# State-space scan: where the input rows of a batch's last eight units come from

## The reference, cut to what matters

```python
def _L0_attn_ref(x, log_lambda, Wd, bd, WB, WC, Wout, bout):
    lam = softplus(log_lambda)                                  # D x N
    delta = softplus(einsum('bld,ed->ble', x, Wd) + bd)
    Bt = einsum('bld,nd->bln', x, WB)
    Ct = einsum('bld,nd->bln', x, WC)
    A_d = exp(-delta[..., None] * lam)                          # b, l, D, N
    B_d = delta[..., None] * Bt[:, :, None, :]
    def step(h, inp):                                           # over l
        a, b, c = inp
        h = a * h + b
        return (h, h * c[:, None, :])
    _, ys = lax.scan(step, zeros((B, D, N)), (A_d, B_d, Ct))
    flat = ys.reshape(B, L, D * N)
    return einsum('blk,dk->bld', flat, Wout) + bout
```

## Time and profile before

| | us |
|---|---|
| median of 3 runs | 4217.18 |
| profiled execution | 4220.45 |
| its span | 4218.7 |
| state-space stage | about 279 to 1120 |
| PE, DVE, POOL, ACT busy between 500 and 600 us | 98.99, 89.12, 74.67, 56.93 |

### The profile page before, as it was taken

The page is one execution under the profiler, slowest core; times in us unless marked ns, Lnnn a source line. Parts: engine busy times, 40 slices in busy tenths (PEclk is TensorE's granted clock), DMA queues, the critical chain, the costliest instruction groups (busy, mean ns, idle before and its releaser), DMA issues. The chain is left out here.

```text
span 4218.7 us, 68490 instructions
## 1 busy us (share of the span) xinstructions
PE 3466.4 (82%) x22579; PEld 2664.5 (63%) x22628; DVE 3413.9 (81%) x6252; ACT 2597.1 (62%) x5081; POOL 1864.5 (44%) x2267
## 2 busy tenths in 40 slices
PE   0149999999689999999999686888868887456998
PEld 0039999999589999999999551111112222446998
DVE  7948888888767777777776777999979887885886
ACT  4745555555344444444444477999979998554665
POOL 5757777777534333343333002222232111464665
PEclk9999999999789999999999675555559999557999
DMA  4334445455422122222222248000011112237986
GB/s 116 106 87 140 139 138 139 138 138 156 120 89 93 65 79 96 96 96 76 68 93 89 63 140 333 22 24 26 26 42 47 47 47 56 73 116 210 274 267 176
DMA packets 288617, 458.27 MB, mean 109 GB/s; under 512 B 45619, under 2 KB 223362, under 8 KB 274814
## 3 DMA queue, kind: packets, MB, share of 16 engines
q1 hardware_dynamic: 268350, 428.16, 33.4%
q0 software_dynamic: 18944, 25.85, 2.1%
q10 hardware_dynamic: 1024, 0.54, 0.1%
HBM read 355.23 MB, written 105.12 MB: 109 GB/s over the span
## 5 line engine op out<-in xcount | busy, mean ns | idle before, releaser
L1056 POOL TENSOR_TENSOR c_ap<-c_ac,c_ap 128x420 fp32r<-128x420 f32 x340 | 405.8, 1194 | 724.5 <-ACT c_ap L1247 724.5
L729 PE MATMUL b_pA<-ab_woutT,b_ys 128*105 128x192 f32 x3840 | 691.7, 327 | 4.8 <-POOL b_ys L567 4.2
L729 PEld LDWEIGHTS b_pA<-ab_woutT,b_ys 128*105 128x105 f32 x3840 | 612.4, 172 | 16.1 <-POOL b_ys L567 5.0
L567 POOL TENSOR_TENSOR b_ys<-b_hs,b_cb 128x525 f32<-128x525 f32 x384 | 506.6, 1320 | 227.3 <-DVE b_hs L794 177.0
L1968 DVE TENSOR_REDUCE g_raw<-g_pS 128x1 f32<-128x525 f32 x816 | 549.5, 703 | 31.5 <-PE g_pS L1923 30.2
L1944 ACT ACTIVATE g_pS<-g_pS,g_stt 128x525 f32<-128x525 f32 x816 | 553.7, 777 | 19.7 <-POOL g_stt L1897 18.8
L1923 PE MATMUL g_pS<-g_qk 16*128 16x262 bf16 (+1 forms) x1536 | 461.5, 408 | 94.1 <-ACT g_pS L1944 35.0
L794 DVE TENSOR_TENSOR_SCAN b_hs<-b_ae,b_pB 128x525 f32<-128x525 f32 x384 | 479.3, 1248 | 43.1 <-ACT b_ae L668 7.3
L1247 ACT ACTIVATE c_ap<-c_ac 128x420 fp32r<-128x420 f32 x340 | 189.3, 557 | 524.8 <-DVE c_ac L1445 522.6
L1129 PEld LDWEIGHTS c_pD<-cw_wd,c_ap 128*105 128x105 f32 x4080 | 424.7, 172 | 30.2 <-POOL c_ap L1056 21.3
L1129 PE MATMUL c_pD<-cw_wd,c_ap 128*105 128x192 f32 x4080 | 436.2, 256 | 9.0 <-POOL c_ap L1056 9.0
(11 more groups left out here) (417 smaller groups left out, 7685.5 us busy)
## 6 DMA issues: line engine op xcount, KB each, us to landing
b_cb<-dram_ct SPq DMA_DIRECT2D x64, 1050.0 KB, 6.1
b_cb<-dram_ct SPq DMA_DIRECT2D x64, 525.0 KB
dram_slots<-g_empty SPq DMA_DIRECT2D x33, 772.0 KB, 21.1
cw_spare<-dram_wt SPq DMA_DIRECT2D x20, 1260.0 KB, 10.4
cw_spare<-dram_wt SPq DMA_DIRECT2D x20, 1050.0 KB, 8.9
cw_spare<-dram_wt SPq DMA_DIRECT2D x20, 840.0 KB, 6.3
m_wo_r<-in_L_ffn_wo_dram SPq DMA_DIRECT2D x24, 576.0 KB
o_wo_r<-in_L_ffn_wo_dram SPq DMA_DIRECT2D x24, 576.0 KB, 5.6
```

The source lines that it names most:

```text
L567: pool.tensor_tensor(ys[:, u % RING, :], hs[:, u % RING, :], cb[:, g % 3, u % GU, :], ALU.mult).then_inc(s["ys"], 1)
L729: ins = pe.matmul(into, ys[:, u % RING, t * TP:(t + 1) * TP], woutT[:, u % NU, :], start=(u == 0 and t % 2 == 0), stop=(u % NU == NU - 1), ...
L1056: nc.gpsimd.tensor_tensor(ap[LO][:, r, :], ac[:, r, :], ap[HI][:, r, :].bitcast(F32), ALU.subtract)\
```

## The change

The tail no longer uses `spread`. `ct` grows from 16 to 48 rows: ACT's copy to `cs`, and its DMA, now take 48 partitions (64 to 111), which hold Bt in fp32 (rows 0 to 15), unused rows, and Ct (rows 32 to 47). A new SBUF buffer `bb` has the eight input rows of the tail, as [128, 2, 4, 525] fp32. SP fills it by four more DMAs per batch of 64 partitions each, two behind the `cb` load of group 2 and two behind that of group 3. In the tail, DVE weighs `bb` in place and scans from it, where it did both on `pB`. In units 0 to 15 nothing of this changes. The wait of `br` (L758 before) is now for the semaphore of the `cs` copy, which follows the `bs` copy on ACT.

```diff
@@ ssm @@
+    INPUT_AT = {2: 0, 3: 1}
+    B0, C0 = 64, 32
...
+        bb = sb("bb", [128, (NU - NS) // GU, GU, S])
...
+                    if g in INPUT_AT:
+                        q = INPUT_AT[g]
+                        for t in range(2):
+                            src = ct_d[b, 2 * q * GU:2 * (q + 1) * GU, :].rearrange("(n t) l -> t n l", t=2)
+                            sp.dma_start(bb[64 * t:64 * t + 64, q, :, :],
+                                         src[t:t + 1].broadcast_to([64, GU, S])).then_inc(s_bb[q], 16)
...
                 if half == 0:
-                    a_eng.wait_ge(s["B"], at(b, NU, -NU))
+                    a_eng.wait_ge(s["B"], at(b, NS, -NS))
                 a_eng.activation(bs[:, k, lo:hi], pF[0:96, 0:hi - lo], ACT.Copy).then_inc(s["b1"], 1)
                 if half == 0:
                     a_eng.wait_ge(s_ct[k], i * 32)
-                a_eng.activation(cs[96:96 + NS, k, lo:hi], pF[96:96 + NS, 0:hi - lo], ACT.Copy)\
+                a_eng.activation(cs[B0:B0 + C0 + NS, k, lo:hi], pF[B0:B0 + C0 + NS, 0:hi - lo], ACT.Copy)\
                     .then_inc(s["faR"], 1)
...
-                a_eng.dma_start(ct_d[b, :, lo:hi], cs[96:96 + NS, k, lo:hi]).then_inc(s_ct[k], 16)
+                a_eng.dma_start(ct_d[b, :, lo:hi], cs[B0:B0 + C0 + NS, k, lo:hi]).then_inc(s_ct[k], 16)
...
-                pe.wait_ge(s["hs"], at(b, NU, u + 1 - 2))
+                pe.wait_ge(s["hs"], at(b, NU, u - 1 if u > 1 else NS - 1 + u - NU))
...
-                    if u < NU - 2:
+                    if u < NS - 2:
                         spread(b, k, u + 2)
-                    elif not last:
+                    elif u >= NU - 2 and not last:
                         spread(b + 1, 1 - k, u + 2 - NU)
...
-                dve.wait_ge(s["b1"], at(b, 2, half + 1))
+                dve.wait_ge(s["faR"], at(b, FS, step + 1))
...
+            def inputs(u):
+                return pB[:, u % 2, OFF:OFF + S] if u < NS else bb[:, (u - NS) // GU, (u - NS) % GU, :]
+
             def weigh(b, k, u):
...
-                dve.wait_ge(s["B"], at(b, NU, u + 1))
-                v.tensor_tensor(pB[:, u % 2, OFF:OFF + S], delta[:, k, 0 if u < NS else 1, :], pB[:, u % 2, OFF:OFF + S],
-                                ALU.mult).then_inc(s["bm"], 1)
+                if u < NS:
+                    dve.wait_ge(s["B"], at(b, NS, u + 1))
+                elif (u - NS) % GU == 0:
+                    dve.wait_ge(s_bb[(u - NS) // GU], b * 32 + 32)
+                x = inputs(u)
+                v.tensor_tensor(x, delta[:, k, 0 if u < NS else 1, :], x, ALU.mult).then_inc(s["bm"], 1)
...
-                    v.tensor_tensor_scan(hs[:, u % RING, :], ae[:, u % RING, :], pB[:, u % 2, OFF:OFF + S], 0.0,
+                    v.tensor_tensor_scan(hs[:, u % RING, :], ae[:, u % RING, :], inputs(u), 0.0,
                                          ALU.mult, ALU.add).then_inc(s["hs"], 1)
```

More of the change, by code:

```diff
@@ L462, in ssm @@
         s_ct = [sem(f"s_ct{k}") for k in range(2)]
+        s_bb = [sem(f"s_bb{q}") for q in range((NU - NS) // GU)]
         s_out = [sem(f"s_out{k}") for k in range(2)]
@@ L494, in body @@
                     if g * GU < NS:
-                        src = ct_d[b, g * GU:(g + 1) * GU, :].rearrange("(a n) l -> a (n l)", a=1)
+                        src = ct_d[b, C0 + g * GU:C0 + (g + 1) * GU, :].rearrange("(a n) l -> a (n l)", a=1)
                         sp.dma_start(cb[:, g % 3, :, :].rearrange("p n l -> p (n l)"),
@@ L500, in body @@
                         for t in range(2):
-                            src = ct_d[b, 2 * j:2 * j + 2 * GU, :].rearrange("(n t) l -> t n l", t=2)
+                            src = ct_d[b, C0 + 2 * j:C0 + 2 * j + 2 * GU, :].rearrange("(n t) l -> t n l", t=2)
                             sp.dma_start(cb[64 * t:64 * t + 64, g % 3, :, :],
                                          src[t:t + 1].broadcast_to([64, GU, S])).then_inc(s_cb[g % 3], 16)
+                    if g in INPUT_AT:
[4 more added lines that the diff above has]
+                                         src[t:t + 1].broadcast_to([64, GU, S])).then_inc(s_bb[q], 16)
                     if g == 3 and not first:
@@ L2997, in trunk @@
                             ssm_lam, ssm_wd, ssm_bd, ssm_wb, ssm_wc, ssm_wout, ssm_bout, W)
-            ssm(nc, h0, W, dram("ct", (NB, 16, S)), h1, early["load"])
+            ssm(nc, h0, W, dram("ct", (NB, 48, S)), h1, early["load"])
         dense_experts(nc, early, dense_held, h1, gate_w, gate_b, gate_bias, wu, bu, wg, bg, wd, bd, swu, sbu, swg, sbg, swd, sbd,
```

## The result

The kernel after takes 4358.5 us (median of 4 runs, 4345.6 to 4391.4) against 4219.9 before. The ratio is 1.0345, with a 95% interval of 1.0310 to 1.0379. I had forecast 4325, in a range of 4285 to 4370. The direction and the mechanism were right; the size was 33 us short, and 4358.5 is also above the forecast's own range, 4300 to 4345. (PE is TensorE, DVE VectorE, ACT ScalarE, POOL GpSimd.) Lines have shifted in kernel.py: the weigh is L802 (was L785), the scan L810 (L794), POOL's ys L577 (L567), the projection L739 (L729), the spread L729 (L719), the front pieces L768 and L777 (L758 and L767), POOL's two others L560 and L551 (L550 and L541).

The account below looks back on a forecast made before the run. Heads were taken as PE-paced, tails as DVE-paced. Fifteen batches at +6.7 us plus 7.4 for the last gave +108, other edits 0: 4220.5 to 4328 profiled, median 4325 us, range 4285 to 4370.

Parts of the forecast that it names:

- PE's 29 us: Tails, 16 batches: eight spreads of 0.23 us each leave PE, 29 us in all, buying almost nothing because DVE is last.
- rival 2: Whole kernel: PE's saved 29 us count in full, giving 4188 us; chance 0.04.
- DVE's wait of 0.61 us for unit 16: Start of each tail: DVE's wait for the spread before its weigh disappears, -0.61 us per batch.
- Two SBUF inputs exclude POOL: Tail: paired weighs and scans take turns with POOL's SBUF work, next starting about 0.14 us before the holder's end; +108 us.
- rival 1: Tail: the scan doesn't exclude POOL, only weigh and ys do; 4207 to 4217 us, most likely 4215; chance 0.10.
- The ledger of a tail: Tail: DVE's and POOL's exclusive holds of 25.0 us plus 0.9 of gaps, 25.9 against 18.6; net +6.7 us per batch.
- steady unit: One tail unit: weigh 0.55, ys 1.16, scan 1.11, gap 0.05, together 2.87 us against 1.94.
- The last batch: Final tail, without front work: eight units at 2.87 us instead of 1.94, +7.4 us.
- POOL's late wait for cb: Batch 15: could shrink by 3 us after a longer tail or grow by a few; counted 0, +-5 in all.
- The other edits: L758's new wait, four more DMAs and the 48-partition copy: 0; the wait bounded by 0.4 us per batch, 6 us.
- rival 3: PE's clock falls in the tail's gaps and each head begins slowly, 2.5 us a batch, +40: 4365 us; chance 0.11.
- My 1.2 us: Tail: PE's predicted idle gaps between pieces of work of 1.6 us, far shorter than 4 us.

Follow-up runs that it names:

- e5: The kernel after, with PE still making the tail's eight spreads into PSUM, where nobody reads them: 4342.6 us, ratio 1.0345.
- e6: The kernel before, with input rows of units 8 to 15 from memory, copied to PSUM by ACT instead of spread by PE: 4217.9 us, ratio 1.0033.
- e3: The kernel before, with only the tail's weigh writing its product to SBUF, so the scan has two SBUF inputs: 4300.0 us, ratio 1.0186.
- e8: The kernel after, with POOL's ys of units 16 to 23 on half the columns: 4285.3 us, ratio 1.0206.
- e2: The kernel after, with the tail's weigh writing to PSUM, so only the weigh has two SBUF inputs: 4318.1 us, ratio 1.0274.
- e7: The kernel after, with POOL's three bias additions moved from units 14, 17, 20 to units 9, 11, 13: 4317.2 us, ratio 1.0284.
- e1: The kernel after with its transfers and waits, but tail spreads back on PE and the broadcast rows unused: 4228.2 us, ratio 1.0025.
- after_again: The kernel after, unchanged, run and profiled again: 4350.8 us, ratio 1.0348.

## Why the prediction was right, and where it was short

1. **Heads PE-paced, tails DVE-paced; PE's 29 us buy nothing.** Right. Keeping the spreads (e5) changes no tail. In a kernel without pairs (e6) the relief is worth 0.9 us a batch, so rival 2's 1.84 (29 us over 16 batches) was too much even there. A spread also costs less than my 0.23 us: eight fewer take 1.3 us off PE's busy time, 0.17 each.
2. **DVE's wait of 0.61 us for unit 16 goes.** Right: heads of 33.00 for 33.62 in the mean of fifteen, -0.62.
3. **Two SBUF inputs exclude POOL, the scan too.** Right, and rival 1 is out: in e3 the scan alone is paired and takes 1.81 us in the median, and in e8 it shortens with POOL's work. The Trainium skill's rule (SBUF — State Buffer, Who interferes with whom) holds for tensor_tensor_scan as for tensor_tensor in this kernel. What I took from it for the length of the block, one instruction, is too short: the loser waited for POOL's whole unbroken run (3.31 us in e2, behind two ys and L560).
4. **The ledger of a tail: 25.9 us.** This is the mis-sized term: 27.17 were measured. Its steady unit of 2.87 was exact (e7). The entry "POOL's L550 behind unit 16, L541 behind units 17 and 20" was too small: it lacked the addition of unit 14, which POOL, coming out of the head with a backlog, does inside the tail, and it assumed that the two engines take turns, where DVE waits for POOL's whole run. Without the three additions the tail is 24.8. They cost 2.35, and I had counted 1.2 for two: 1.15 of the missing 1.3. Over 15 batches the period grew by 15 x 7.97 = 119.5 us instead of 101. The last batch gave only 0.5 instead of 7.4. Up to its last scan its tail grew by 7.3, as the ledger has it. But before, PE still had 27 records of projections to start when that scan ended, and after only 14, so 1.4 us of it went again: 5.9. And its head shrank by 5.4, because DVE's waits there, 5.3 us before (3.3 for spreads, the 0.6 of step 2 among them, and 2.0 for ys), are none after. They stand behind POOL's late wait for cb, 7.6 us before and 4.3 after, which I had allowed for in words (3 us) and not in the sum. Stage: +120, forecast +108.
5. **The other edits: 0.** In the kernel after nothing of them is seen. With DVE at its old pace L768's wait costs 5.9 us, the bound given (e1).
6. **The clock (rival 3).** It fell, and it cost nothing. The timeline of PE at the tail's end:

```profile
578.04 0.62 PE L729 MATMUL b_pB<-b_bs,ab_sel 96*128 96x263 bf16 x2 [4.82 <-DVE b_bs L777]
578.45 3.41 PE L739 MATMUL b_pA<-ab_woutT,b_ys 128*105 128x192 f32 x10
...
581.65 0.65 PE L729 MATMUL b_pB<-b_bs,ab_sel 96*128 96x263 bf16 x2
```

The granted clock is 0.87 in the tail and 1.00 in the head. The short gaps did not do it: from 564 to 572 us, with gaps of 0.2 and 1.6, it is 1.00. It fell in a gap of 4.8, to 0.53 from 578 to 583, near the lower of its two levels (1.2 of 2.4 GHz), and is 1.00 again from 583 to 590. My 1.2 us had missed that gap: PE's queue stands at the next batch's spread, which waits for DVE's L777, itself blocked (1.83 for 0.42). The slow projection of 3.41 us lies where DVE sets the pace: between 577 and 584 us DVE has one wait, 0.2 us for ACT, and none for PE.

7. **What stands beyond the stage.** Of the 139 us between the medians 120 are the stage's. The stages behind it differ between profiles of any of these kernels (2702 to 2725 us for the part ahead of the last stage), and the kernel after has one run in four some 50 us above the others. The remaining 10 to 20 us (19 here; 10 by the medians of after_again, 4350.8 and 4220.7) are put down to these two, which is argued, not shown. How often a run stands apart does differ with the kernel: 20 of 62 with broadcast input rows, 2 of 68 of the kernel before.
8. **The range.** It held by luck. The forecast's own range ended at 4345; 4358.5 lies in the part that was put on for rival 3, the clock, and the clock cost nothing. What filled it were step 4 and step 7.

## What to carry to other kernels

Before an operand of VectorE moves from PSUM to SBUF, list what GpSimd does at that time: in these runs two SBUF inputs turned the engines' overlap into a sum, and VectorE paid for GpSimd's whole unbroken run, backlog included. Time taken from an engine that looks 99% busy is worth only what a wait on it was worth where it is taken: 0.6 us here, for 8.6 us of new blocking. And a copy by a third engine that repairs this has to stand in that engine's queue ahead of anything that waits.

## What the runs showed of the hardware that was not expected

- POOL's operations back to back leave no seam: a paired DVE instruction of 0.69 us waited through two ys and L560 (3.31 us), and a scan of 1.25 took 3.06. To be issued first did not help: the weigh at 565.73 let a ys issued at 566.49 go first.
- With weigh alone paired the tail grows by 5.5 us, with the scan alone by 4.6, with both by 8.6: the prices don't add. That whichever goes first is covered by the other's wait is my reading, not shown.
- In the last stage DVE's instruction is issued 0.26 us ahead of POOL's and is still second (4020.91 and 4021.17, 3.79 us for 0.96). Why POOL wins there isn't shown. The first bullet would fit: DVE's instruction before it ends at 4020.99, and POOL's before, the indirect DMA L2928, at 4021.15, so POOL leaves hardly a seam there either. But no run shows that L2928 holds what the two share.
